# Delta stage: filter taps moved to VectorE, masks made a level ahead, statistics taken branch by branch

## The reference, cut to what matters

```python
v = silu(_causal_dwconv(hs @ Wv, conv_w_v))       # q, k alike, 4 taps
inv = solve_triangular(eye + A, eye)              # A = strict lower part of kb @ k.T
u = inv @ v;  delta_out = attn @ u_i              # chunked in the reference
local_short = fir(vh, fir_short_w)                # 5 taps on each channel
local_long = fir(vh, fir_long_w)                  # 64 taps on each channel
stats = concat([_stats(local_short), _stats(local_long), _stats(delta_out), _stats(vh)])  # mean, var, mean abs, norm
hgate = gelu(concat([hs_exp, stats]) @ mlp_w1 + mlp_b1)
probs = softmax((hgate @ mlp_w2 + mlp_b2) / temp) * (1.0 - 2.0 * FLOOR_EPS) + floor
o = probs[0]*local_short + probs[1]*local_long + probs[2]*delta_out + probs[3]*vh + sigmoid(conv_res_logit)*local_short
out = rmsnorm(o) @ Wo
```

## Time and profile before

| | us |
|---|---|
| median of 3 runs | 1656.15 (1654.65 to 1660.35) |
| the profiled execution, its own time | 1649.57 |
| its span in the profile | 1647.8 |
| delta stage in it, first norm statistics to `x` | 1277.0 to 1388.1 |
| granted TensorE clock, mean over the span | 0.948 |

### The profile page before, as it was taken

One profiled execution on the slowest core, in us unless ns is written; L12 is line 12 of the kernel. 1 busy time (PEld: TensorE's weight loads), 2 busy tenths in 40 slices (PEclk: granted clock), 3 DMA queues, 4 the chain that ended last, 5 costly groups with the idle time before them and its releaser, 6 DMA issues. The chain is left out here.

```text
span 1647.8 us, 29080 instructions
## 1 busy us (share of the span) xinstructions
PE 1446.8 (88%) x11204; PEld 1088.0 (66%) x11204; DVE 926.8 (56%) x2764; ACT 762.1 (46%) x1782; POOL 91.8 (6%) x86
## 2 busy tenths in 40 slices
PE   7999989976499858899999999999997876768996
PEld 6978979853277643467777777777775872546765
DVE  5654455554676312377777777777775453453434
ACT  6744535423122200266666666666665941212222
POOL 2300000000000200200000000000000000000000
PEclk9999999977799979999999999999999996899999
DMA  9945424111232479600100001001000302206860
GB/s 336 336 151 203 146 81 144 67 39 66 83 134 90 156 278 367 233 35 35 35 35 35 35 35 35 35 35 35 2 1 2 125 1 118 108 0 211 278 252 4
DMA packets 63464, 181.19 MB, mean 110 GB/s; under 512 B 7264, under 2 KB 43232, under 8 KB 62048
## 3 DMA queue, kind: packets, MB, share of 16 engines
q1 hardware_dynamic: 59488, 160.18, 26.8%
q0 software_dynamic: 3264, 12.58, 1.9%
q10 hardware_dynamic: 576, 6.58, 1.0%
HBM read 178.68 MB, written 0.66 MB: 109 GB/s over the span
## 5 line engine op out<-in xcount | busy, mean ns | idle before, releaser
L1916 ACT ACTIVATE cross_s<-cross_s,cross_shift 128x896 f32<-128x896 f32 x224 | 215.1, 1031 | 38.7 <-DVE cross_shift L2000 38.7
L1910 ACT COPY cross_eT<-cross_ring 128x512 f32<-128x512 f32 x280 | 153.1, 591 | 143.4 <-PE cross_ring L1838 143.4
L1838 PEld LDWEIGHTS cross_ring<-consts,cross_s 128*128 128x128 f32 x1568 | 168.2, 141 | 56.3 <-issue 44.2
L1838 PE MATMUL cross_ring<-consts,cross_s 128*128 128x128 f32 x1568 | 197.0, 277 | 6.1 <-ACT cross_s L1916 6.1
L1991 DVE CUSTOM_DVE_ANT_0 cross_s<-cross_scores,cross_mask,cross_top 128x448 f32<-128x448 f32 x224 | 141.3, 681 | 84.8 <-PE cross_scores L1830 84.7
L436 ACT ACTIVATE slots_probs<-slots_scores,slots_bias,ctx_rinv 128x128 f32<-128x128 f32 x294 | 130.1, 462 | 108.1 <-DVE slots_bias L484 108.1
L1991 DVE CUSTOM_DVE_ANT_0 cross_s<-cross_scores,cross_mask,cross_half_max 128x448 f32<-128x448 f32 x224 | 141.4, 680 | 13.3 <-PE cross_scores L1830 13.3
L155 PE MATMUL slots_scores<-slots_qkT,slots_ctxT 128*128 128x128 f32 x1176 | 138.3, 275 | 7.9 <-DMA slots_ctxT<-in_ctxT 7.1
L155 PEld LDWEIGHTS slots_scores<-slots_qkT,slots_ctxT 128*128 128x128 f32 x1176 | 136.8, 192 | 11.9 <-DMA slots_ctxT<-in_ctxT 8.1
L386 PE MATMUL slots_attended<-ctx_rows,slots_probs 128*128 128x257 f32 x588 | 135.2, 380 | 1.2 <-DVE slots_pooled L498 1.1
L1830 PE MATMUL cross_scores<-cross_keysT,cross_qz 32*128 32x448 f32 x896 | 121.8, 588 | 3.9 <-DVE cross_half_max L1991 2.7
(11 more groups left out here) (774 smaller groups left out, 2116.0 us busy)
## 6 DMA issues: line engine op xcount, KB each, us to landing
slots_ctxT<-in_ctxT SPq DMA_DIRECT2D x42, 896.0 KB, 4.6
ctx_rows<-in_ctx_rows SPq DMA_DIRECT2D x28, 896.0 KB, 7.8
ring_w<-in_moe_w POOLq DMA_DIRECT2D x12, 1024.0 KB, 16.4
ring_w<-in_moe_w SPq DMA_DIRECT2D x12, 1024.0 KB, 10.5
cross_ctxT<-in_ctxT SPq DMA_DIRECT2D x13, 896.0 KB, 4.5
padded_ctxT<-in_ctxT SPq DMA_DIRECT2D x12, 896.0 KB, 4.5
plain_ctxT<-in_ctxT SPq DMA_DIRECT2D x12, 896.0 KB, 4.6
local_layers<-in_w_local SPq DMA_DIRECT2D x2, 4806.0 KB, 14.3
```

Of the source, the lines that this page charges most:

```text
L1838: last = pe.transpose(bank(("turn", u, t))[:, j * P:(j + 1) * P], s_buf[:, u % 2, j, t * P:(t + 1) * P], K.ident)
L1910: act.copy(eT[:, u % 2, t], bank(item)).then_inc(st("emptied_act"), 1)
L1916: act.activation(rows, rows, ACT.Exp, bias=shift[:, u % 2, j:j + 1], scale=SCALE).then_inc(st("exp"), 1)
```

## The change

- 36 taps leave PE and ACT: the 10 short ones and the last 26 long ones of the second half of the channels. DVE computes each as a multiply-add over 128 elements (`tap_some`), between its other work in levels 1 to 5. Three products with the identity add the sums to bank 7 in level 6. Each waits for the one before it (`link`).
- `E` has two buffers. The mask of level n+1 is made right behind the copy of `EI` of level n; that of level 1 ahead of the first `inv`.
- The corrections are made in two groups of four: first `inv`, then its transpose, with semaphores of their own. The next level's first product waits for `inv` alone.
- PE's taps now go 28 ahead of the levels, 5 and 4 in each level, and none is left behind `u`.
- Statistics are taken by branch: those of `v` in levels 1 to 3, those of the filters while `u` and the delta output are made, those of the delta output last, read from PSUM. The branches `v` and delta swap places in `z`, and rows and columns of the gate's weights are swapped on the host to match.
- The gate's products with `hT` stand ahead of the wait for the statistics, in banks 0 and 2; Gelu starts on the first half while PE makes the second.
- In the softmax, bias and temperature are applied by one instruction, and the scale and both additions by two; what these need is made beforehand.

```diff
+VECTOR_LONG = 26
+
+
...
-    return [(kind, c, k) for kind, rows, length in (("conv", 3 * DC, CONV), ("long", DC, LONG), ("short", DC, SHORT))
-            for c in range(rows) for k in range(length)]
+    taps = [("conv", c, k) for c in range(3 * DC) for k in range(CONV)]
+    taps += [("long", c, k) for c in range(DC) for k in range(LONG - (VECTOR_LONG if c == DC - 1 else 0))]
+    return taps
+
+
+def vector_taps():
+
+    return [("short", c, k) for k in range(SHORT) for c in range(DC)] + [("long", DC - 1, k) for k in range(LONG - VECTOR_LONG, LONG)]
...
-        E = st.sb("E", [P, HEADS4, P])
+        E = st.sb("E", [P, 2, HEADS4, P])
+        short_sum = st.sb("short_sum", [P, DC, P])
+        long_sum = st.sb("long_sum", [P, P])
+        floors = st.sb("floors", [P, HEADS4, 4])
+        bias2 = st.sb("bias2", [P, 16])
...
+        gate_in = [b[i][:, :].rearrange("p (h k) -> p h k", k=P) for i in (0, 2)]
...
+                filter_some(28)
                 for n in range(1, LEVELS):
                     pe.wait_ge(st("E"), n)
+                    pe.wait_ge(st("inv"), n)
                     for hd in range(HEADS4):
-                        last = pe.matmul(b[4][:, hd * P:(hd + 1) * P], E[:, hd], inv[:, 0, hd], start=True, stop=True)
+                        last = pe.matmul(b[4][:, hd * P:(hd + 1) * P], E[:, n % 2, hd], inv[:, 0, hd], start=True, stop=True)
                     last.then_inc(st("EI_mm"), 1)
-                    filter_some(4)
+                    filter_some(5)
                     pe.wait_ge(st("EI"), n)
+                    pe.wait_ge(st("inv_rows"), n)
                     for hd in range(HEADS4):
-                        pe.matmul(b[5][:, hd * P:(hd + 1) * P], inv[:, 1, hd], EI[:, hd], start=True, stop=True)
+                        last = pe.matmul(b[5][:, hd * P:(hd + 1) * P], inv[:, 1, hd], EI[:, hd], start=True, stop=True)
+                    last.then_inc(st("IEI_mm"), 1)
+                    for hd in range(HEADS4):
                         last = pe.matmul(b[6][:, hd * P:(hd + 1) * P], EI[:, hd], inv[:, 1, hd], start=True, stop=True)
-                    last.then_inc(st("IEI_mm"), 1)
-                    filter_some(8)
-                pe.wait_ge(st("inv"), LEVELS)
+                    last.then_inc(st("IEI_rows_mm"), 1)
+                    filter_some(4 if n < LEVELS - 1 else len(taps_in_turn))
+                    if n == LEVELS - 1:
+                        pe.wait_ge(st("taps"), 1)
+                        pe.matmul(b[7][:, D + P:2 * D], long_sum[:, :], K.ident, start=False, stop=True)
+                        for c in range(DC):
+                            last = pe.matmul(b[7][:, c * P:(c + 1) * P], short_sum[:, c], K.ident, start=True, stop=True)
+                        last.then_inc(st("filters_mm"), 1)
+                pe.wait_ge(st("inv_rows"), LEVELS)
                 for hd in range(HEADS4):
...
                 last.then_inc(st("u_mm"), 1)
-                filter_some(len(taps_in_turn))
                 pe.wait_ge(st("u"), 1)
...
                 last.then_inc(st("delta_mm"), 1)
-
+                for c in range(DC):
+                    for k in range(DC):
+                        pe.matmul(gate_in[c], w1[:, k, c * P:(c + 1) * P], hT[:, k].unsqueeze(1).to_broadcast([P, HEADS4, P]),
+                                  start=k == 0, stop=False)
...
                 for c in range(DC):
-                    cols = slice(c * P, (c + 1) * P)
-                    last = product(pe, b[c][:, :].rearrange("p (h k) -> p h k", k=P),
-                                   [(w1[:, k, cols], hT[:, k].unsqueeze(1).to_broadcast([P, HEADS4, P])) for k in range(DC)]
...
+                    pe.matmul(gate_in[c], W["w1s"][0:GATE_IN, c * P:(c + 1) * P], statsT[:, :], start=False, stop=True).then_inc(st("gate_mm"), 1)
+                pe.wait_ge(st("gateT"), DC)
...
-                act.wait_ge(st("gate_mm"), 1)
                 for c in range(DC):
-                    last = act.activation(gateT[:, c], b[c][:, :], ACT.Gelu, bias=W["b1"][:, c:c + 1])
-                last.then_inc(st("gateT"), 1)
+                    act.wait_ge(st("gate_mm"), c + 1)
+                    act.activation(gateT[:, c].rearrange("p (h k) -> p h k", k=P), gate_in[c], ACT.Gelu, bias=W["b1"][:, c:c + 1]).then_inc(st("gateT"), 1)
...
+                def tap_some(count):
...
+                    for kind, c, k in itertools.islice(tap_places, count):
...
+                        if k == (0 if kind == "short" else LONG - VECTOR_LONG):
+                            link(dve.tensor_scalar(total, vT[:, c, lo:lo + P], taps_of[kind][:, c, k:k + 1], None, ALU.mult))
+                        else:
+                            link(dve.scalar_tensor_tensor(out=total, in0=vT[:, c, lo:lo + P], scalar=taps_of[kind][:, c, k:k + 1], in1=total,
+                                                          op0=ALU.mult, op1=ALU.add))
...
+                def sums(part, rows):
+
+                    dve.tensor_reduce(flat3(msq[:, part]), rows, X_AXIS, ALU.add, apply_absolute_value=True)
+                    link(dve.tensor_reduce(flat3(mean[:, part]), rows, X_AXIS, ALU.add))
+                    dve.tensor_scalar(stat(2, part), msq[:, part], 1.0 / HEAD64, None, ALU.mult)
+                    link(dve.tensor_scalar(mean[:, part], mean[:, part], 1.0 / HEAD64, None, ALU.mult))
+                    dve.tensor_copy(stat(0, part), mean[:, part])
...
+                def squares(part, rows):
+
+                    apart = zz[:, part].rearrange("p a h d -> p (a h) d")
+                    link(dve.tensor_tensor(apart, rows, spread(flat3(mean[:, part]), HEAD64), ALU.subtract))
+                    link(dve.tensor_tensor(apart, apart, apart, ALU.mult))
+                    dve.tensor_tensor(mean[:, part], mean[:, part], mean[:, part], ALU.mult)
+                    link(dve.tensor_reduce(flat3(var[:, part]), apart, X_AXIS, ALU.add))
...
+                def rest(part):
+
+                    link(dve.tensor_scalar(var[:, part], var[:, part], 1.0 / HEAD64, None, ALU.mult))
+                    return dve.tensor_tensor(msq[:, part], mean[:, part], var[:, part], ALU.add)
...
+                filters, own, found = slice(0, 2), slice(2, 3), slice(3, 4)
...
+                dve.tensor_tensor(E[:, 1], A[:, 1], repeat(joinT[:, 1], HEADS4), ALU.mult).then_inc(st("E"), 1)
                 link(dve.tensor_tensor(inv[:, 0], A[:, 0], repeat(join[:, 0], HEADS4), ALU.mult))
                 link(dve.tensor_tensor(inv[:, 1], A[:, 1], repeat(joinT[:, 0], HEADS4), ALU.mult))
-                link(dve.tensor_tensor(inv[:, 0], ident4, inv[:, 0], ALU.subtract))
-                dve.tensor_tensor(inv[:, 1], ident4, inv[:, 1], ALU.subtract).then_inc(st("inv"), 1)
-                dve.wait_ge(st("inv"), 1)
+                dve.tensor_tensor(inv[:, 0], ident4, inv[:, 0], ALU.subtract).then_inc(st("inv"), 1)
+                dve.tensor_tensor(inv[:, 1], ident4, inv[:, 1], ALU.subtract).then_inc(st("inv_rows"), 1)
+
+                def edges(n):
+                    dve.tensor_tensor(E[:, n % 2], A[:, 1], repeat(joinT[:, n], HEADS4), ALU.mult).then_inc(st("E"), 1)
+
                 for n in range(1, LEVELS):
-
-                    dve.tensor_tensor(E[:, :], A[:, 1], repeat(joinT[:, n], HEADS4), ALU.mult).then_inc(st("E"), 1)
+                    tap_some(1)
                     dve.wait_ge(st("EI_mm"), n)
                     dve.tensor_copy(EI[:, :], two(b[4][:, :])).then_inc(st("EI"), 1)
+                    if n + 1 < LEVELS:
+                        edges(n + 1)
+                        tap_some(3)
+                    if n == 1:
+                        sums(own, rows_of(own))
...
+                        squares(own, rows_of(own))
...
+                        rest(own).then_inc(st("own"), 1)
+                        tap_some(4)
...
+                        tap_some(5)
...
+                        tap_some(len(vector_taps()))
+                        dve.memset(marks[:, 2:3], 0.0).then_inc(st("taps"), 1)
+                    dve.wait_ge(st("inv_rows"), n)
                     dve.wait_ge(st("IEI_mm"), n)
-                    link(dve.tensor_tensor(inv[:, 0], inv[:, 0], two(b[5][:, :]), ALU.subtract))
-                    dve.tensor_tensor(inv[:, 1], inv[:, 1], two(b[6][:, :]), ALU.subtract).then_inc(st("inv"), 1)
-                    dve.wait_ge(st("inv"), n + 1)
+                    dve.tensor_tensor(inv[:, 0], inv[:, 0], two(b[5][:, :]), ALU.subtract).then_inc(st("inv"), 1)
+                    dve.wait_ge(st("IEI_rows_mm"), n)
+                    dve.tensor_tensor(inv[:, 1], inv[:, 1], two(b[6][:, :]), ALU.subtract).then_inc(st("inv_rows"), 1)
+                dve.wait_ge(st("filters_mm"), 1)
+                link(dve.tensor_copy(z[:, 0:2].rearrange("p a h d -> p (a h d)"), b[7][:, :]))
                 dve.wait_ge(st("u_mm"), 1)
                 dve.tensor_copy(u[:, :], b[1][:, 0:D]).then_inc(st("u"), 1)
-                dve.wait_ge(st("filtered"), len(taps_in_turn))
```

(31 more changed lines are left out.)

51 lines of the change are left out of this document (26 added, 25 removed).

## The result

The changed kernel takes 1649.93 us (median of 8 runs, 1646.64 to 1651.41), the kernel before 1658.78 us in the same comparison (8 runs, 1653.17 to 1662.29). The ratio is 0.995, with a 95% interval of 0.9936 to 0.9963: 0.005 of 1658.8 is 8.3 us less, between 6.1 and 10.6. The forecast was 11.4 us less and 1644.8 us, with a range of 1639.0 to 1651.0. It was set against the 1656.15 us of the first three runs of the kernel before; the median of eight is 2.6 us higher, so about half of the 5.1 us between 1644.8 and 1649.93 is this baseline.

The account below looks back on a forecast made before the run. Levels looked PE-bound (34.4 of 36.8 us), partly gap-filling taps; DVE chains and the gate's low PE clock also cost time. Gains 1.1 + 3.5 + 6.2 + 0.6 = 11.4 us off 1656.15 gave 1644.8, range 1639.0 to 1651.0.

Parts of the forecast that it names:

- softmax: In the softmax: three small steps fewer, each 0.17 us and a link, 0.6 us gained.
- Ahead of the levels: Before level 1: PE's 28 taps end last, so PE starts at 1310.0, a gain of 0.2 us.
- The levels: Six levels: DVE ends levels 1 to 5, 30.9 us against 31.1; with the start, 1.1 us gained.
- Level 6: Last level: nothing left for DVE, 4.8 us to the start of `u`.
- Rival 2: Levels: DVE dearer than priced (1648.8 us), or clock falls in level 5's idle 2.4 us, 2.7 us more; chance 0.17.
- sign of being wrong: Levels: the prediction is wrong if they together take longer than before.
- From `u` to the statistics: From `u` to the turning: taps gone and a quarter of the statistics already taken, 9.6 us against 13.1, 3.5 gained.
- The gate: Turning to softmax: products with `hT` hidden, the rest at the low clock, 10.3 us against 16.5, 6.2 gained.
- rival 1: Gate: the clock holds throughout, so it takes 6.4 us, another 3.9 gained, 1640.9 us in all; chance 0.22.
- Rival 3: Last filter taps or a DVE step hold up `u` or the statistics; under 5 us gained, about 1652; chance 0.05.
- Rival 4: Levels: the clock falls in level 1 and stays low; 5.5 us slower than before, 1661.7; chance 0.02.
- The other signs of being wrong: PE still at products with `hT` when statistics are ready, or time off this stage moving by more than 3 us.

Follow-up runs that it names:

- e2: Changed kernel with each level's mask made behind the subtractions of the level before; ratio to the kernel before 0.9962.
- e11: Changed kernel with six idle products ahead of the wait for the activated v and four in level 5; ratio to the kernel before 0.9927.
- e9: The kernel before the change, profiled again with nothing changed; ratio to the kernel before 0.9992.
- e1: Changed kernel with all 138 taps back on PE, none on DVE; ratio to the kernel before 0.9928.
- e6: Changed kernel with 22 taps on DVE instead of 36; ratio to the kernel before 0.9911.
- e5: Changed kernel with idle products on PE in the gate's gaps (six, one and one); ratio to the kernel before 0.9928.
- e10: Changed kernel with both correction groups interleaved again and the next level's first product behind both subtractions; ratio to the kernel before 0.9956.
- e8: The changed kernel itself, run and profiled once more; ratio to the kernel before 0.9956.
- e3: Changed kernel with the gate's four products with `hT` behind the statistics again; ratio to the kernel before 0.9946.
- e4: Changed kernel with the statistics of all four branches taken together behind the delta output; ratio to the kernel before 0.9949.

## Why the prediction was right, and by how much it was off

The time lies in the range, and the direction and the place of the gain were right. The sum said 11.4 us and 8.3 were measured. With two profiles of each kernel, its terms stand as follows (us, gain positive; measured is the difference of the two means):

```
                      forecast   before          changed         measured
start to level 1        0.2      33.2, 35.7      35.5, 35.5       -1.1
levels 1 to 6           0.9      36.7, 36.7      37.0, 37.0       -0.3
u to the turning        3.5      13.0, 13.0       9.3,  9.3        3.7
turning to softmax      6.2      16.5, 13.4       8.7, 10.1        5.6
softmax                 0.6       2.4,  2.4       1.8,  1.8        0.6
stage                  11.4     111.6, 111.0    102.1, 103.4       8.5
```

**Ahead of the levels.** The step itself is right: PE's 28 taps ended last, and PE, not DVE, started level 1. Without a fall of the clock it took 33.0 to 33.1 (e2, e11) against 33.2, as the 0.2 forecast has it. The measured -1.1 is one fall in two profiles before against two in two after, and e9 shows that the kernel before has it too. It says nothing of the change.

**The levels.** The forecast for levels 1 to 5 was 5.5, 5.8, 6.2, 6.3 and 7.1; measured were 5.43, 5.88, 6.19, 6.37 and 7.22. A tap was priced at 0.345 and took 0.350. Level 6 is the step that failed: forecast 4.8 at the full clock, measured 5.93, with the clock at 0.50 for most of it. Rival 2 had said what could happen here, 2.4 idle us in level 5 and a low clock behind them, and gave it 2.7 us. It happened in both profiles of the changed kernel, at 1.2 us, since the clock came back before level 6 was over. With the clock held (e11) the six levels take 35.8 us, 0.1 from the sum's 35.7. That the levels gain so little was forecast, but the prediction named as a sign of being wrong that they take longer than before together, and they do, by 0.3 us (37.0 and 36.7). The gain in the whole comes from behind the levels alone.

The Trainium skill's warning ("VectorE: DVE Perf Modes", on the TRN2 errata: many small tiles pay the fixed latency each time) pointed the right way. A tap cost 0.35 us on DVE against 0.22 on PE, and e1 and e6 show that 36 are too many and none too few. The prediction's estimate by that page's formula should be 1.7 us and not 1.8: 31 times the difference of 0.345 and 0.291.

**From `u` to the statistics.** 9.28 against a forecast 9.6. The reductions came as priced, at 0.68 us for 512 elements and 0.42 for 256. The other 0.3 us weren't split up; unlinked steps, which overlap, would make it shorter.

**The gate.** 10.3 was forecast, and 8.7 and 10.1 were measured, so the low clock that was chosen is close to the second profile; rival 1, the clock held through all of it, came true only in part and in one of the two. With idle products in the gaps (e5) the stretch took 6.3 us, which is rival 1's 6.4. The larger error is in the term it was set against: the kernel before takes 16.5 or 13.4 us here, by whether the clock rises between its products, and one profile showed only the first. That is 1.6 us of the forecast's excess on the mean, against 0.9 that the changed kernel's own gate came in lower.

The Trainium skill's page "TensorE: Matmul & The Clock Gate" (HAM oscillation) says that a long enough idle gap brings the lower clock back. The traces agree for the longer gaps: the clock fell in all six of 4.0 to 4.3 us at the start and in both of 8.0 us ahead of the turning in the kernel before. The shorter gaps can't be priced by it. The gap of 3.0 us ahead of the turning kept the full clock in four of seven profiles (changed, e1, e6, e10; not e2, e8, e11), the 2.3 us in level 5 kept it in one of five, and in e2 the clock fell behind a gap of 1.95 us.

**The other rivals.** Rival 3 fell: no filter tap and no DVE step other than the last subtraction holds `u` up, as `u` starts 0.05 us behind it. Rival 4 fell as well: with PE's share down to 79% in levels 1 to 5 the clock stayed at 1.00 over all of them.

**The other signs of being wrong.** PE was done with the products with `hT` 3.0 us before the statistics were ready. The time off this stage was to move by no more than 3 us, and it moved by 8.9 between the first two profiles. That sign can't tell anything here, since it moved by 7.2 us between two profiles of the kernel before as well (1536.2 and, in e9, 1543.4). By the medians of the runs it did not move: they differ by 8.85 us, and the two means of the stage by 8.5.

The size of the miss owes something to chance. Of the shortfall of 2.9 us in the stage (8.5 against 11.4), 1.3 lie at the start, whose falls are not the change's, and 1.1 in level 6. In the gate two errors, of 1.6 and 0.9 us, in part cancel.

What stays open is the total of single parts in the time of the whole kernel. The ratios to the kernel before are 0.9962 (e2), 0.9946 (e3), 0.9949 (e4), 0.9956 (e8) and 0.9956 (e10), with intervals of 0.004 to 0.005 that overlap; e9, the kernel before itself, has 0.9992. Those parts are told apart by the trace alone, with one profile for each kernel.

## What to carry to other kernels

Before moving work to an idle engine, add up both engines' work for each step of the loop. Here, with the hand-overs shortened, 36 taps on VectorE made it the bound of the levels (31.1 us for five), none made it TensorE (29.0), and 22 split the work evenly (25.8). Let the product of the next step wait for the one operand that it needs (0.6 us a level here). Before hiding products or opening gaps, look at what runs behind them: a fall of the clock cost 1.2 us in level 6 and nothing in a level that VectorE ends. Compare stages, not spans, where the spread of the runs is as large as the effect.

## What the runs showed of the hardware that was not expected

- The clock's falls come and go between executions of the same code, and an earlier rise can bring a later fall. Where the clock rose 5.7 to 6.0 us into the stage, PE got ahead, waited 4.0 to 4.3 us for the same `vT`, and lost the clock: 35.5 to 35.7 us to level 1 in six profiles, against 33.0 to 33.2 in four where it rose later. In the three kernels with six idle products there it was 33.0 to 33.1 each time.
- Two unlinked steps on DVE overlap: the second subtraction starts 0.61 us behind the first, which lasts 0.69 (1344.12 and 1344.73 above). Linked, as before, it was 0.72.
- A multiply-add with a scalar by partition takes 0.06 us more on DVE than a plain step on two tensors of 128 elements, 0.35 against 0.288.
